# Moving every third state product of a selective scan from VectorE to GpSimd, and folding the layer norms, in a decoder layer on one core

## The chip, the cores and the metric

The kernel runs on one core of a Trainium2 chip. The metric is the device time of one execution in microseconds; the times of several runs are given by their median. The core has TensorE (PE, matrix products into PSUM), VectorE (DVE), ScalarE (ACT), GpSimd (POOL) and SyncE (SP, which here only issues DMAs). Each engine works through its own list of instructions in order and waits on semaphores.

## What is computed

One decoder layer in fp32, batch 4, length 512, width 512, with three residual branches:

```python
x = x + attn(_layernorm(x))                  # chunked linear attention, 16 heads of 32
x = x + mixer(ctx_1024, _layernorm(x))       # selective scan, gated by silu of the normed x
x = x + ffn(_layernorm(x))                   # bit-linear feed-forward, hidden 2048
# the mixer's recurrence, 16 states n for each of 512 channels:
dA    = exp(dt * A);  state = state * dA + (dt * u) * B[n];  y = sum_n(state * C[n])
y     = (y + D * u) * silu(z)
# bit_linear: rows of x are scaled by 127 / max|x| and rounded before the product
```

## The kernel before

Each batch row b (0 to 3 in the code; the text says rows 2 to 4 for b = 1 to 3) goes through a front (input projection, convolution, step sizes dt), the scans with the attention beside them, and the mixer gate and feed-forward. `step(b, f)` on every engine interleaves the scans and the attention of row b with the mixer end and feed-forward of row f = b - 1; `first_row` and `last_row` are the ends. The order on each engine is written out: the tables `STEP_PIECES` (VectorE's halves of a unit), `STEP_DECAYS` (ScalarE) and `STEP_SPREADS` (TensorE) say how many pieces of the recurrence are taken at each named point of the list.

A *unit* is one state n for one half h of the channels, 128 partitions x 2 x 512 columns; there are 32 per row, `unit(u)` gives (b, h, n) of unit u = 32 b + j. In rows b = 1 to 3 the order is states 0 to 5 of half 0, then states 6 to 15 with both halves one after the other (`joined`: the second uses the same B and C rows), then states 0 to 5 of half 1: 22 distinct rows of B and C for 32 units. For each unit:

- ScalarE forms the decay exp(dt A) into one of four DEC buffers (L1353).
- TensorE broadcasts B's row n to 128 partitions into a PSUM bank of PB by a product (L1060), once for each distinct row, when the scan that used the bank before is done.
- VectorE multiplies DU (dt u) by it into PSUM (`inputs_b`, L1893) and then scans: W = scan(decay, PB) (`scan`, L1904). W is a ring of four SBUF buffers; scan u waits until the transfer of unit u - 4 has landed.
- SyncE loads C's row n as a broadcast into one of two CROW buffers (`c_row`), two units ahead.
- GpSimd multiplies W by it in place (`outputs_c`, L1730), waits until the transfer before has landed (`y_summed`) and issues the DMA that adds W to ACC in SBUF (L1743). In row b = 0 two units are added first. GpSimd also forms DU (`step_inputs`, L1751), splits B for the broadcast product (`split`), and adds the output bias after unit 7 of a row (`bias`, L1718).

Norms. The next row's input is normed by VectorE in attention group 3: bn_stats (L1835), aggregation (L1841), ScalarE's reciprocal root (`rstd`), then four in-place tensor_scalar (`normed`, L1848), transposed by TensorE. The mixer's gate needs the mean and variance of X1 right after the residual additions (`residual`, L2104; `mixer_sums`; `aggregate(f, 1)`; `gate_shift`; ScalarE's `gate_z`, L1405), and then VectorE multiplies ACC by it (`gate_mixer`, L2115; in the last row `gate_tile`, L1966). For the feed-forward `add_mixer` (L2120) forms X2, bn_stats follow, `normed` writes OT, and `row_scales` (in the last row `tile_scales`) takes the largest magnitude (L2009, L1977) for the rounding.

## Time and profile before

| | us |
|---|---|
| median of 3 runs | 931.2 (930.08 to 934.58) |
| profiled execution, its own time | 933.21 |
| its span | 931.4 |

| engine | busy us | share |
|---|---|---|
| TensorE, matrix products | 791.9 | 85% |
| VectorE | 780.5 | 84% |
| ScalarE | 584.6 | 63% |
| GpSimd | 489.2 | 53% |

The span is the time from the first to the last instruction of the profiled execution. A share of busy time is an average over stages; an engine below 100% may still be the one that everything waits for in a stage. In rows of the trace "out<-in" names the tiles with buffer numbers left out, and an arrow in brackets names what ended the idle time before an instruction.

### The profile page before, as it was taken

How to read it: one execution, taken by the hardware profiler on the slowest of the kernel's cores; microseconds unless marked ns; L12 is line 12 of the kernel's file. 1: busy time of each engine (PE TensorE's matmuls, PEld its weight loads, DVE VectorE, ACT ScalarE, POOL GpSimd, SP SyncE). 2: the span in 40 equal slices, each digit the busy share in tenths (PEclk: the TensorE clock that was granted, in tenths of full speed). 3: DMA queues.
4: the chain of work that ended last, by engine and by line, in shares of the span. 5: the costliest groups of instructions: out<-in, count | busy, mean ns of one | idle time of the engine just before them, and what ended most of it. 6: DMA issues, size and time to landing. Idle time of an engine off the chain costs nothing. (4 is left out here: it accounts for less than half of the span.)

```text
span 931.4 us, 11695 instructions
## 1 busy us (share of the span) xinstructions
PE 791.9 (85%) x4070; PEld 429.4 (46%) x4070; DVE 780.5 (84%) x913; ACT 584.6 (63%) x868; POOL 489.2 (53%) x292
## 2 busy tenths in 40 slices
PE   5859898369887888998978987998889899999798
PEld 1334555143452334665443333656445335664343
DVE  5887788996998986989699988589788998988875
ACT  3788899965647866445365866453455796453552
POOL 0456678786646523575447643276444755565020
PEclk8889997679789999989999999989998999999999
DMA  8687788866546535666534563456643565666000
GB/s 291 252 247 224 229 251 225 238 187 165 122 96 133 114 69 113 143 144 169 125 68 113 121 140 68 111 130 149 158 98 79 123 126 130 151 144 135 1 12 34
DMA packets 50781, 131.12 MB, mean 141 GB/s; under 512 B 7298, under 2 KB 7874, under 8 KB 50724
## 3 DMA queue, kind: packets, MB, share of 16 engines
q0 software_dynamic: 16128, 58.73, 33.4%
q1 hardware_dynamic: 34596, 71.65, 23.8%
q8 instruction: 33, 0.54, 0.2%
q14 instruction: 24, 0.20, 0.1%
HBM read 67.09 MB, written 4.35 MB: 77 GB/s over the span
## 5 line engine op out<-in xcount | busy, mean ns | idle before, releaser
L1730 POOL TENSOR_TENSOR W<-W,CROW 128x1024 f32<-128x1024 f32 x128 | 321.9, 2531 | 160.1 <-DVE W L1904 132.6
L1904 DVE TENSOR_TENSOR_SCAN W<-DEC,PB 128x1024 f32<-128x1024 f32 x125 | 285.1, 2281 | 10.2 <-ACT DEC L1353 4.0
L1743 POOL DMA_DIRECT2D ACC<-W x112 | 98.3, 878 | 155.1 <-DMA ACC<-W 132.0
L1893 DVE TENSOR_TENSOR PB<-DU,PB 128x1024 f32<-128x1024 f32 x128 | 156.5, 1223 | 13.7 <-PE PB L1060 10.1
L1353 ACT ACTIVATE DEC<-DT,ACOL 128x511 f32<-128x511 f32 x250 | 160.1, 710 | 11.5 <-DVE W L1904 11.4
L1116 PE MATMUL bank<-W,ARENA 128*128 128x512 fp8e4 x512 | 124.0, 386 | 0.0
L1308 ACT ACTIVATE ARENA<-bank 128x512 f32<-128x512 f32 x56 | 32.5, 592 | 73.4 <-PE bank L876 36.4
L1116 PEld LDWEIGHTS bank<-W,ARENA 128*128 128x128 bf16 x512 | 45.3, 98 | 61.2 <-issue 16.9
L1451 ACT ACTIVATE ARENA<-bank,SDQ 128x512 f32<-128x512 f32 x64 | 43.4, 685 | 46.0 <-PE bank L1116 45.8
L1060 PE MATMUL PB<-BC,ID 96*128 96x512 bf16 x98 | 39.3, 415 | 33.7 <-DVE W L1904 32.4
L876 PE MATMUL bank<-XNT,WK 128*128 128x512 f32 x128 | 63.7, 644 | 2.2 <-DVE ARENA L1936 2.2
L1936 DVE TENSOR_TENSOR ARENA<-bank,CAUSAL 128x512 f32<-128x512 f32 x64 | 42.5, 680 | 24.4 <-PE bank L977 24.3
L938 PEld LDWEIGHTS bank<-WV,XNT 128*128 128x128 f32 x512 | 60.5, 195 | 3.2 <-issue 2.2
L2044 DVE SCALAR_TENSOR_TENSOR ARENA<-bank,SDQ,ARENA 128x512 f32<-128x512 f32 x64 | 47.3, 743 | 17.3 <-PE bank L1116 6.6
L876 PE MATMUL bank<-XNT,WQ 128*128 128x512 f32 x128 | 61.4, 624 | 0.0
L938 PE MATMUL bank<-WV,XNT 128*128 128x128 f32 x512 | 61.2, 278 | 0.3 <-ACT ARENA L1440 0.3
L1132 PE MATMUL bank<-W,ARENA 128*128 128x512 fp8e4 x256 | 57.9, 379 | 0.0
L1109 PE MATMUL bank<-BROW,RT 32*128 32x512 bf16 x128 | 30.2, 388 | 23.7 <-DVE ARENA L2044 14.0
L1860 DVE SCALAR_TENSOR_TENSOR U<-bank,CW,U 128x511 f32<-128x511 f32 (+2 forms) x48 | 35.5, 747 | 15.1 <-ACT U L1315 13.8
L1751 POOL TENSOR_TENSOR DU<-DT,U 128x512 f32<-128x512 f32 x16 | 22.9, 1506 | 47.2 <-ACT DT L1333 47.2
L1440 ACT ACTIVATE ARENA<-bank 128x512 bf16<-128x512 int16 x76 | 40.5, 594 | 11.0 <-PE bank L918 10.9
L876 PE MATMUL bank<-ARENA,FM 128*128 128x512 f32 x96 | 45.5, 609 | 0.0
(175 smaller groups left out, 1333.2 us busy)
## 6 DMA issues: line engine op xcount, KB each, us to landing
ACC<-W POOLq DMA_DIRECT2D x112, 512.0 KB, 4.6
CROW<-c_rows SPq DMA_DIRECT2D x98, 256.0 KB, 3.6
W<-in_wffn SPq DMA_DIRECT2D x27, 512.0 KB, 6.2
X<-in_wffn SPq DMA_DIRECT2D x21, 512.0 KB, 5.8
X<-in_x SPq DMA_DIRECT2D x7, 1024.0 KB, 8.6
out_dram<-X SPq DMA_DIRECT2D x16, 256.0 KB, 2.2
X<-in_ctxT SPq DMA_DIRECT2D x4, 512.0 KB, 5.6
ARENA<-in_x SPq DMA_DIRECT2D x1, 1024.0 KB, 5.6
```

What stands on the lines that cost most here:

```text
L876: last = pe.matmul(o, lhs, rhs, start=start, stop=n == len(terms) - 1)
L938: last = pe.matmul(o[:, t * P:(t + 1) * P], XNT[:, k, t * P:(t + 1) * P], WV[:, k, g * P:(g + 1) * P], start=k == 0, stop=k == KT - 1)
L1116: last = pe.matmul(o, XQT[:, k, t * P:(t + 1) * P], w, start=False, stop=k == KT - 1)
L1132: last = pe.matmul(o, HT[:, k, :], W8[:, 2 * WPC + k // 2, (k % 2) * 512:(k % 2) * 512 + 512], start=k == 0, stop=k == HK - 1)
L1353: last = act.activation(to[:, i, 1:], DT[:, e, 1:], ACT.Exp, scale=ACOL[:, e, n:n + 1])
L1451: act.activation(G[n % 2], R.bank(f, "G", t, c)[:, :], ACT.Silu, scale=SDQ[:, 0, t:t + 1])\
L1730: pool.tensor_tensor(w, w, CROW[k % 2][:, :].unsqueeze(1).broadcast_to([P, 2, L]), ALU.mult)\
L1743: pool.dma_start(ACC[accumulator(u)][:, :, :], w, accum_op=ALU.add).then_inc(y_summed, 16)
L1893: dve.tensor_tensor(into, du, rows, ALU.mult).then_inc(dbu_done.sem, 1)
L1904: dve.tensor_tensor_scan(flat(W[u % 4]), flat(decay_of(u)), flat(PB[:, scan_bank(u):scan_bank(u) + 2, :]), 0.0, ALU.mult, ALU.add).then_in ...
L1936: dve.tensor_tensor(homes(b, g)["st"][c % 2].rearrange("p (h q) -> p h q", h=HPG), R.bank(b, "S", g, c)[:, :].rearrange("p (h q) -> p h q" ...
L2044: dve.scalar_tensor_tensor(h, R.bank(f, "V", t, c)[:, :], SDQ[:, 1, t:t + 1], G[(t * HC + c) % 2], ALU.mult, ALU.mult)\
```

## The change

In rows b = 1 to 3 every third distinct row of B is handled by GpSimd: SyncE loads it as a broadcast row from DRAM into one buffer BRW (`b_row`, four units ahead; B rows are now stored to DRAM beside C's), GpSimd multiplies DU by it straight into W (`inputs_b` on GpSimd, two units ahead of its multiplication by C), and VectorE scans W in place. TensorE's broadcast and VectorE's product fall away for those 10 of 32 units of a row. The other units keep their way; the tables that order the pieces are as before.

The norms: the next input is normed on ScalarE by a scaled Identity. The mixer's mean comes from the residual addition itself (tensor_tensor_reduce, with the sum), the variance from a ScalarE Square with accumulation. Before the feed-forward, `add_mixer` also keeps the row minimum, and the normalisation also keeps its maximum, so that the largest magnitude needs no reduction of its own. Small tiles are packed together, and the bias columns lie in ARENA, which changes no instruction.

```diff
+POOL_EVERY = 3
+POOL_AHEAD = 2
+ROW_AHEAD = 4
+def on_pool(u):
+    return u >= UNITS and (ROW_OF[u] - ROW_OF[u // UNITS * UNITS]) % POOL_EVERY == POOL_EVERY - 1
...
+        BRW = sb("BRW", [P, L])
...
+            def b_row(u):
+                if u >= TOTAL or not on_pool(u) or joined(u):
+                    return
+                b, _, n = unit(u)
+                k = POOL_ROW[u]
+                sp.wait_ge(*bc_stored.at(b))
+                if k > 1:
+                    sp.wait_ge(pool_dbu_done, BY_POOL[LAST_IN_POOL_ROW[k - 1]])
+                sp.dma_start(BRW[:, :], bc_rows[b, n].partition_broadcast(P)).then_inc(b_loaded, 16)
...
-                sp.dma_start(c_rows[b], XBC[N:2 * N, :]).then_inc(c_stored.sem, 16)
+                sp.dma_start(bc_rows[b], XBC[0:2 * N, :]).then_inc(bc_stored.sem, 16)
...
+                    b_row(b * UNITS + j + ROW_AHEAD)
                     if b * UNITS + j + 2 < TOTAL:
                         c_row(b * UNITS + j + 2)
...
-                    if not joined(u):
+                    if not joined(u) and not on_pool(u):
                         spread_b(u)
...
+            def deviations(f, t):
+                act.wait_ge(*mean_ready.at(f, t + 1))
+                act.activation(Z[:, t, :], X1[:, t, :], ACT.Square, bias=NMEAN[:, t:t + 1],
+                               accum_out=VAR[:, t:t + 1]).then_inc(var_ready.sem, 1)
...
+            def normed(b):
+                act.wait_ge(*xshift_ready.at(b))
+                for t in range(TT):
+                    act.activation(XROWS[b][:, t, :], XROWS[b][:, t, :], ACT.Identity, bias=XSHIFT[:, t:t + 1],
+                                   scale=RSTD[0][:, t:t + 1]).then_inc(xn_ready.sem, 1)
...
+            def inputs_b(u):
+                b, h, n = unit(u)
+                if opens(u):
+                    pool.wait_ge(*du_ready.at(b, 2 * h + 2))
+                if u - 4 < PAIRED and u % 2 == 0:
+                    pool.wait_ge(pair_added, (u - 4) // 2 + 1)
+                else:
+                    pool.wait_ge(y_summed, 16 * transfers(u - 4))
+                pool.wait_ge(b_loaded, 16 * POOL_ROW[u])
+                pool.tensor_tensor(W[u % 4][:, :, :], DU[:, 2 * h:2 * h + 2, :],
+                                   BRW[:, :].unsqueeze(1).broadcast_to([P, 2, L]), ALU.mult).then_inc(pool_dbu_done, 1)
...
             for u in range(TOTAL):
+                if u + POOL_AHEAD < TOTAL and on_pool(u + POOL_AHEAD):
+                    inputs_b(u + POOL_AHEAD)
                 outputs_c(u)
...
+            def normed_peak(f, t):
+                dve.tensor_tensor_reduce(OT[:, t, :], X2[:, t, :], MV[1][:, t, 0:1].broadcast_to([P, D]),
+                                         RSTD[1][:, t:t + 1], -LARGEST, ALU.subtract, ALU.max, HIGH[:, t:t + 1])\
+                   .then_inc(xn2_ready.sem, 1)
...
+            def scan_in_place(u):
+                dve.wait_ge(pool_dbu_done, BY_POOL[u])
+                dve.wait_ge(*da_ready.at(0, u + 1))
+                dve.tensor_tensor_scan(flat(W[u % 4]), flat(decay_of(u)), flat(W[u % 4]), 0.0,
+                                       ALU.mult, ALU.add).then_inc(scan_done.sem, 1)
...
-                    if n % 2:
+                    if n % 2 and on_pool(n // 2):
+                        scan_in_place(n // 2)
+                    elif n % 2:
                         scan(n // 2)
-                    else:
+                    elif not on_pool(n // 2):
                         inputs_b(n // 2)
...
-                dve.tensor_reduce(AMX[:, :], OT[:, :, :], AX.X, ALU.max, apply_absolute_value=True)\
-                   .then_inc(q_step.sem, 1)
+                dve.wait_ge(*deep_step.at(f))
+                dve.tensor_tensor(AMX[:, :], DEEP[:, :], HIGH[:, :], ALU.max).then_inc(q_step.sem, 1)
...
-                dve.tensor_tensor(X1[:, t, :], R.bank(f, "wo", t)[:, :], X1[:, t, :], ALU.add)\
+                dve.tensor_tensor_reduce(X1[:, t, :], R.bank(f, "wo", t)[:, :], X1[:, t, :], 1.0, 0.0,
+                                         ALU.add, ALU.add, TOTALS[:, t:t + 1])\
...
-                dve.tensor_tensor(X2[:, t, :], R.bank(f, "yT", t)[:, :], X1[:, t, :], ALU.add)\
+                dve.tensor_tensor_reduce(X2[:, t, :], R.bank(f, "yT", t)[:, :], X1[:, t, :], 1.0, LARGEST,
+                                         ALU.add, ALU.min, LOW[:, t:t + 1])\
...
-            def mixer_sums(f, t):
+            def mixer_mean(f, t):
                 dve.wait_ge(*R.drained_at(f, "wo", t))
-                sums(f, 1, X1, t)
+                dve.tensor_scalar(NMEAN[:, t:t + 1], TOTALS[:, t:t + 1], -1.0 / D, None, ALU.mult)\
+                   .then_inc(mean_ready.sem, 1)
```

## Rows read from the trace of the kernel before

**Rows 1.** Busy time by stage: from, to, length, then each engine, clock, DMA share.
```profile
229.80:458.00 228.20, 198.83 (x1020) 107.94 (x1019) 196.60 (x218) 130.55 (x196) 125.34 (x78) 0.95 0.57 125
458.00:678.00 220.00, 194.27 (x1003) 106.31 (x1002) 185.81 (x203) 129.39 (x194) 113.20 (x72) 0.93 0.53 117
678.00:851.40 173.40, 160.59 (x938) 91.61 (x937) 158.37 (x176) 106.28 (x157) 97.26 (x59) 0.98 0.57 124
851.40:931.40 80.00, 69.78 (x361) 31.09 (x359) 57.09 (x137) 36.79 (x61) 9.08 (x7) 0.98 0.11 27
```

**Rows 2.** The chain of waits from 527 to 931 us, by line, as shares.
```profile
by line: PE bank L876 17.2%; PE bank L1116 10.5%; issue 6.5%; PE bank L1017 5.2%; PE bank L1132 5.2%; DVE W L1904 5.0%; PE bank L938 4.5%; PE bank L977 3.4%; PE bank L1000 2.9%; DVE PB L1893 2.9%; DVE HAM L2052 2.6%; DVE BST L1835 2.5%; PE 
```

**Rows 3.** Pieces of the same chain in order of time: start, length, what.
```profile
643.58 1.84 DVE X L1848 x3
645.55 2.96 issue
682.11 1.19 DVE BST L1835 x2
```

**Rows 4.** Who waited for whom, GpSimd, 229 to 852 us: total, times, longest.
```profile
POOL ACC L1743 <- DMA ACC<-W: 125.1, 64, 6.1
POOL W L1730 <- DVE W L1904: 119.5, 31, 14.0
POOL ACC L1743 <- POOL W L1730: 14.3, 26, 0.6
```

**Rows 5.** Groups of instructions: shapes, count, busy us, mean ns, idle before.
```profile
L1730 POOL TENSOR_TENSOR W<-W,CROW 128x1024 f32<-128x1024 f32 x128 | 321.9, 2531 | 160.1 <-DVE W L1904 132.6 <-DMA CROW<-c_rows 27.5
L1904 DVE TENSOR_TENSOR_SCAN W<-DEC,PB 128x1024 f32<-128x1024 f32 x125 | 285.1, 2281 | 10.2 <-ACT DEC L1353 4.0 <-issue 3.0 <-DMA ACC<-W 1.0
L1893 DVE TENSOR_TENSOR PB<-DU,PB 128x1024 f32<-128x1024 f32 x128 | 156.5, 1223 | 13.7 <-PE PB L1060 10.1 <-issue 2.1
L1060 PE MATMUL PB<-BC,ID 96*128 96x512 bf16 x98 | 39.3, 415 | 33.7 <-DVE W L1904 32.4 <-DVE BC L1877 1.3
```

**Rows 6.** Timeline of VectorE and GpSimd near 245 us: start, length, what.
```profile
244.67 3.42 DVE L2115 TENSOR_TENSOR ARENA<-ACC,ARENA 128x1024 f32<-128x1024 f32 x2
245.09 4.13 POOL L1751 TENSOR_TENSOR DU<-DT,U 128x512 f32<-128x512 f32 x2 [2.62 <-ACT DT L1333]
```

**Rows 7.** Groups of the norms; the last is a line's durations, minimum/median/maximum.
```profile
L1835 DVE BATCH_NORM_STATS2 BST<-X 128x6 f32<-128x512 f32 x44 | 28.8, 681 | 0.3
L1848 DVE TENSOR_SCALAR X<-X,MV,RSTD 128x512 f32<-128x512 f32 x12 | 13.4, 1172 | 0.0
L2104 DVE TENSOR_TENSOR X<-bank,X 128x512 f32<-128x512 f32 x16 | 10.8, 678 | 13.2 <-PE bank L1023 13.2
L1848 DVE TENSOR_SCALAR OT<-X,MV,RSTD 128x512 f32<-128x512 f32 x12 | 7.2, 661 | 0.0
L2009 DVE TENSOR_REDUCE AMX<-OT 128x4 f32<-128x2048 f32 x3 | 6.8, 2283 | 0.1
L1491 ACT ACTIVATION_READ_ACCUMULATOR W<-W 128x1 f32 x18 | 3.4, 189 | 0.0
L1393 ACT ACTIVATE OT<-bank x16: 576/588/597, 104.2 to 843.6; 128x512 f32<-128x512 f32 x16
```

**Rows 8.** Timeline around the bias addition of step b = 2.
```profile
497.11 0.88 POOL L1743 DMA_DIRECT2D ACC<-W  x1 [0.54 <-issue]
497.71 4.81 POOL L1718 TENSOR_TENSOR X<-X,OUTB 128x2048 f32<-128x2048 f32 x1
507.23 2.29 DVE L1904 TENSOR_TENSOR_SCAN W<-DEC,PB 128x1024 f32<-128x1024 f32 x1
```

**Rows 9.** Timeline of GpSimd, its last two DMA issues.
```profile
851.51 0.88 POOL L1743 DMA_DIRECT2D ACC<-W  x1 [1.53 <-DMA ACC<-W]
856.29 0.88 POOL L1743 DMA_DIRECT2D ACC<-W  x1 [1.52 <-DMA ACC<-W]
```

**Rows 10.** Timeline of VectorE in the last row, the gate's second pair.
```profile
862.79 1.40 DVE L1966 TENSOR_TENSOR ARENA<-ACC,ARENA 128x512 f32<-128x512 f32 x2 [1.39 <-ACT ARENA L1405]
```

More of the change, by code:

```diff
@@ L615, in homes @@
             return at
+        BIAS, BREST = (part((HID // 64) * i, HID // 64) for i in range(2))
+        BPART = part(HID // 32, 3 * HID // 128, bf16).rearrange("p (j n) -> p j n", j=3)
         BCR = X1[0:32, 0, :]
@@ L1526, in attention @@
                         square(b, g - 1)
+                    if b + 1 < BATCH and g == GROUPS - 1:
+                        normed(b + 1)
                     decays(b, "a", g, 1)
@@ L1568, in first_row @@
                 rstd(0, 0)
+                normed(0)
                 act.wait_ge(setup_v, SETUP_V - 2)
@@ L1601, in step @@
                     decays(b, "r", 2)
+                for t in range(TT):
+                    deviations(f, t)
                 rstd(f, 1)
@@ L1680, in last_row @@
                 for pair in range(2):
+                    for t in (2 * pair, 2 * pair + 1):
+                        deviations(f, t)
                     rstd_tiles(f, 1, 2 * pair, 2 * pair + 2)
@@ L2145, in attention @@
                     units(b, "a", g, 0)
+                    if b + 1 < BATCH and g == GROUPS - 1:
+                        norm_shift(b + 1)
                     feature(b, g, 1)
                     units(b, "a", g, 1)
[L2148 to L2149 removed]
                     units(b, "a", g, 2)
@@ L2232, in step @@
                 feature(b, 0, 1)
-                normed(f, 2, X2, xn2_ready)
+                normed_peaks(f)
                 units(b, "v", 9)
```

167 lines of the change are left out of this document (94 added, 73 removed).

## The prediction, made before any run of the changed kernel

> **What bounds the kernel now.** I read the busy time by stage first, then the chain of waits, then who waits for whom, then single durations. The stages [rows 1] are the steps that interleave the scans of row b with the feed-forward part of row b-1: 228.2, 220.0 and 173.4 us for b = 1, 2, 3, then 80 us of the last row alone. Over the three steps (621.6 us) TensorE is busy 553.7 us, VectorE 540.8, ScalarE 366.2, GpSimd 335.8. Neither of the first two is full; each waits for the other in turn. The chain that ended last says which of them matters where: from 527 us on, its lines [rows 2] are mostly TensorE's; added up over its listed pieces, TensorE holds 219 of those 404 us and VectorE 81. So a microsecond taken off TensorE there is worth roughly 0.6, one off VectorE 0.2 to 0.3, unless it lies where VectorE is the chain. Such places exist: around the norms [rows 3] the chain runs through VectorE. By contrast in the last attention stretch (790 to 851 us) VectorE holds 3 us of the chain and TensorE 54.
>
> GpSimd looks idle, but its chain is stiffer than its busy share. It waits 125.1 us for its own accumulating transfers and 119.5 us for scans between 229 and 852 us [rows 4]. Each transfer into ACC waits for the one before; in a backlog the issues are 4.78 us apart [rows 9] whatever GpSimd does. 32 units at that pace are 153 us of a step.
>
> **Part 1, a third of the products moved to GpSimd.** Of the 22 distinct states per row, numbers 2, 5, 8, 11, 14, 17, 20 move: 2 + 6 + 2 = 10 of 32 units, 30 in all, with 21 of TensorE's B broadcasts.
> - VectorE loses 30 products of 1223 ns [rows 5], 36.7 us.
> - TensorE loses 21 x 0.415 us [rows 5] = 8.7 us.
> - GpSimd gains 30 products shaped like its multiplication by C, 2.53 us [rows 5]: 76 us. In a backlog its cycle is 4.78 us, of which 1.52 is waiting before the issue [rows 9]; 0.55 of that (14.3 us in 26 waits [rows 4]) would remain as the wait for its own multiplication. So about 1.0 us of a new product hides and 1.4 lengthens the chain: 14 us a row if it were always in backlog.
> - The scan in place now reads both inputs from SBUF. The only VectorE instructions of the trace with that trait are the two Z products (L2115). At 244.67 us such a pair took 3.42 us [rows 6], where two products of that size are 2.4 [rows 5], while GpSimd's pair of 512-column products beside it took 4.13 us, where half the size of two multiplications is 2.5: one engine waits until the other's instruction ends, in both directions. The Trainium skill (SBUF — State Buffer, Who interferes with whom) says this as a rule: a VectorE instruction with two SBUF inputs contends with a GpSimd instruction that reads SBUF, and the second to issue blocks fully. By that rule, the trace agrees. This speaks against the change. GpSimd will be in a reading instruction about (336 - 84 + 76)/610 = 54% of the time (84 us being its 96 DMA issues of 0.88 us [rows 9]); the mean remainder of 2.5 us is 1.25 us, so 0.67 us per scan; since GpSimd often starts just behind a scan, I take 0.8 us: 24 us for 30 scans. Bounds: 0, and a whole multiplication each, 30 x 2.53 = 76 us. A scan that only reads other memory keeps its 2.28 us.
> - New waits. VectorE's scan in place waits for GpSimd's product, with all of VectorE's list (masks, features, gated products, and behind them TensorE) behind it. GpSimd forms it two units ahead, before multiplication u. Mostly it is done 2 to 4 us before the scan. The exception is after GpSimd's 4.81 us bias addition in step b = 2 [rows 8]: it ends at 502.5, then product 74 (2.4), multiplication 72 (2.4), an issue (0.6) and product 75 (2.4) end near 510, where the scan of unit 75 starts at 507.2 now [rows 8]: 3 us, and some 1 us at 74. In b = 1 and 3 scans are later relative to the bias. The wait for the ring (scan u waits for transfer u-4; that of unit 75 for the issue of 497.11, landed some 4.6 us later, 5.5 us before the scan [rows 8]) has 5 to 10 us to spare in most attention stretches, paired in this way, and is eaten by chain delays of 5 to 9 us there.
> - SyncE: 21 broadcast loads of a B row (256 KB each) go ahead of the C row loads. Their own wait, for the previous GpSimd row's product, is older than the wait of the C row queued behind it, so it holds up nothing; the store of 32 rows instead of 16 costs nothing visible. If a load is late, GpSimd's whole queue waits for it; in b = 1 and 2 it sits, like the C row of unit 20, behind a result store.
>
> On the path: products, L1893 holds 2.9% of the 404 us of chain [rows 2], 11.7 us, of some 52 products (65 us) run in it, 18%; so -36.7 x 0.18 = -6.6. Blocking: L1904 holds 5.0%, 20 us of some 121, 17%: +24 x 0.17 = +4.1. Broadcasts: -8.7 x 0.62 = -5.4. Sum -7.9.
>
> **Part 2, the norms.**
> - The next input's normalisation (L1848, X<-X) leaves VectorE: 12 instructions, 13.4 us [rows 7], a mean of 1172 ns because some sat blocked beside GpSimd; at 643.5 us they and the gap of 2.96 us hold the chain for 5.3 us [rows 3]. The same four cost ScalarE about 0.6 to 0.8 us each (its Square: 588 ns median [rows 7]), beside VectorE's work; ScalarE is busy only 59% in the steps [rows 1]. On the path I take half: -6.7 for three rows.
> - Statistics of the mixer's input: 16 of the 44 bn_stats (681 ns [rows 7], 0.60 apart [rows 3]) and 16 aggregations go, 16 means of some 0.15 us come, ScalarE adds 16 squares of 0.59 us with an accumulator read of 0.19 [rows 7]. At the start of a step the chain has two bn_stats and the aggregation behind the last residual [rows 3], 1.19 + 0.4 us; in their place come one mean, one square and its read, 0.9: -0.7 each, and about -0.3 each for the shorter run of residuals. -3 for three steps, nothing in the last row, where one bn_stats is traded for one square.
> - Rounding scale: the normed X2 (12 in 7.2 us) and the maximum over 2048 (3 of 2283 ns [rows 7]) become four instructions with a row maximum. No tensor_tensor_reduce is in the trace. Nearest rows: a tensor_tensor of 512 columns is 0.68 us [rows 7]; the scan needs 2.28 us where a product of its size needs 1.22 [rows 5], so 1.2 us is the other end. An accumulator read may add up to 0.19 us (ScalarE's). I take 0.78. Per step 4.7 us become 3.1 + 0.4 of small ones + 0.7 blocked (its mean operand is in SBUF too): -0.5, three times -1.5. Last row: 0.60 (7.2/12) and a quarter of 2.28 become 0.78 + 0.15, four times: -1.
> - The residual and mixer additions gain the reduction as well: 32 x 0.1 = 3.2 us of VectorE, on the path +1.2.
> Sum -11.
>
> **Part 3, what GpSimd gives back.** Step b = 2: +2 of the 4 us of waiting. At the end of b = 3 GpSimd's last issue is at 856.29 [rows 9], lands near 861 (the previous one left at 851.51 and the wait for it ended just before 856.29), and VectorE needs ACC at 862.79 [rows 10]: 1.9 us of slack. Four of the last twelve units (units 22, 23, 27, 30 of the row) are GpSimd's, 4 x 1.4 = 5.6 us, less the slack and an earlier start: +3. Late scans at the ends of b = 1 and 2: +2. Sum +7.
>
> Total -7.9 - 11 + 7 = -12. The profiled execution took 933.2 (span 931.4), 2 us above the median of 931.2, so its forecast is 921 and the median's 919.
>
> **The rivals.**
> - *Slower: GpSimd's chain becomes the bound.* Each moved unit costs the 1.4 us above and 1.8 of the 2.3 us during which a scan in place can hold GpSimd off, 3.2 us. In each row's attention stretch some four such units stand where GpSimd never waits for a scan: 13 us less 6 of slack in the ring, +7 for b = 1 and 2, and at the very end without slack, 7 + 7 + 13 = +27 in place of my +7: 939. It decides from about 2.8 us (12 units x 2.8 less 14 of slack is the 19 us gained elsewhere) of chain per moved unit. For: the cadence of 4.78 us is already met at the end of b = 3 [rows 9]. Against: 119.5 us of waiting for scans [rows 4]. Chance 0.15.
> - *Hidden anyway.* VectorE's savings fall where TensorE ends last, as in 790 to 851 us. Then only the broadcasts (-5.4) and some 4 us of norms count, against +7: 929. Chance 0.14.
> - *The reducing form takes two cycles per column.* 48 instructions x 0.55 = 26 us of VectorE, 40% on the path, +10: 929. The Trainium skill (Vector Engine (DVE) Microarchitecture Reference, Points that are easy to get wrong) says that the accumulating form with two SBUF sources that aren't bf16 runs at half rate; no row shows that form. That would strike only the 16 of the normed X2, in place of all 48. Chance 0.07.
> - *No blocking.* If scans in place meet a free GpSimd, the 4.1 and most of the 7 vanish, and freed VectorE time starts later work sooner: 907. Chance 0.06.
> - *It does not do what it says*, the products arriving after the scan wants them, ends in the slower rival, whose 0.15 holds it.
>
> **How the numbers follow.** The forecast, 906 to 926, has 0.58. The bounds: blocking from 0 to 76 us is -4 to +9 on the path, the reducing form up to +10, GpSimd's part 0 to +20, the norms -20 to -5. Range 902 to 938. A change under 0.5% (926.5 to 935.9) can't be told from none. Faster: 0.58 + 0.06 less the forecast's own edge 0.02, 0.62. Same: 0.14 + 0.07, 0.21. Slower: 0.15 + 0.02, 0.17.
>
> **What would show it.** Scans in place: 2.28 us where GpSimd is quiet, 3 to 4.9 where it isn't, mean about 3.1; any that stay at 2.28 throughout refute the blocking. GpSimd busy near 560 us, its wait for scans well under 119.5. VectorE busy near 745, TensorE near 783. tensor_tensor_reduce at 0.7 to 0.8 us. VectorE waiting for a GpSimd product near unit 75 and hardly elsewhere. The last ACC transfer later relative to the last scan. The prediction is wrong if the reducing form is slow, if waits for the product are frequent, or if the steps b = 1 and 2 shrink by over 10 us each.

## The result and the profile after

The changed kernel takes 972.8 us (median of 4 runs, 969.45 to 975.81) where the kernel before took 932.6 on the same chip: ratio 1.043, interval 1.040 to 1.046. It was forecast at 919, with a range up to 938. It is 40 us slower, and the forecast missed in sign. Two kernels below had one slow execution (3379 us beside 941 to 948 for the norms alone, 952 beside 938 to 944 without GpSimd's products), which their medians leave out here and which the 944.9 and 941.2 in later expectations hold.

First the busy time of the engines, from the page of the changed kernel (span 969.5 us):

```profile
PE 804.8 (83%) x4049; PEld 434.0 (45%) x4049; DVE 769.3 (79%) x906; ACT 607.6 (63%) x916; POOL 569.6 (59%) x322
```

VectorE lost 11 us of work, not the 35 forecast; TensorE, with 21 broadcasts fewer, is busy 13 us longer. Then the stages, cut at the first residual addition of a row (columns as in [rows 1]: TensorE's products, its weight loads, VectorE, ScalarE, GpSimd, granted clock, DMA share, GB/s; the first line is row 1):

```profile
0.00:239.10 239.10, 173.44 (x755) 93.96 (x756) 180.27 (x176) 186.94 (x268) 147.35 (x81) 0.83 0.77 226
239.10:474.40 235.30, 198.14 (x1004) 108.36 (x1003) 194.31 (x209) 136.66 (x208) 151.80 (x87) 0.91 0.57 127
474.40:702.70 228.30, 198.84 (x1003) 107.11 (x1002) 181.03 (x205) 134.87 (x206) 136.06 (x79) 0.92 0.52 118
702.70:885.80 183.10, 164.74 (x931) 93.10 (x930) 159.92 (x177) 109.25 (x165) 122.77 (x70) 0.94 0.57 126
885.80:969.50 83.70, 69.62 (x360) 31.43 (x358) 53.74 (x144) 39.92 (x69) 11.67 (x9) 0.96 0.14 32
```

[Rows 1] end their first three stages at 458, 678 and 851.4; here they end at 474.4, 702.7 and 885.8. Row 1 ended at 229.8 and now ends at 239.1. So every stage lost: 9 us in row 1, 34.4 - 9.3 = 25 in the three steps, 4 in the tail. (In the kernel before, the first residual addition of row 2 is at 454.5, not at the 458 where [rows 1] cut; with that cut the steps grew by 10.5, 4.7 and 9.8 us.) The loss of row 1 comes with the norms: its end is at 237.2 with the norms alone and at 230.5 with the products alone, the two kernels of the next section. TensorE's granted clock was 0.93 to 0.98 in the steps [rows 1] and is 0.91 to 0.94, and its busy time there rose from 554 to 562 us. I take that for an effect of the waiting; no run separates the two. The instructions that answer to [rows 5], and the new ones (L2004 is the scan in place, L1817 GpSimd's product):

```profile
L1792 POOL TENSOR_TENSOR W<-W,CROW 128x1024 f32<-128x1024 f32 x128 | 325.4, 2558 | 126.1 <-DVE W L1997 94.0 <-DMA CROW<-bc_rows 18.4 <-DVE W L2004 13.7
L1997 DVE TENSOR_TENSOR_SCAN W<-DEC,PB 128x1024 f32<-128x1024 f32 x95 | 216.7, 2281 | 15.2 <-DMA ACC<-W 5.4 <-ACT DEC L1395 4.5 <-POOL W L1803 2.7
L2004 DVE TENSOR_TENSOR_SCAN W<-DEC,W 128x1024 f32<-128x1024 f32 x30 | 106.9, 3562 | 15.3 <-POOL W L1817 14.7 <-ACT DEC L1395 0.6
L1817 POOL TENSOR_TENSOR W<-DU,BRW 128x1024 f32<-128x1024 f32 x30 | 81.5, 2717 | 4.7 <-DMA BRW<-bc_rows 4.7
```

A scan in place takes 3562 ns on average, one from PSUM 2281. Of GpSimd's 132.6 us of waiting for scans [rows 5] 108 are left. The chain of waits between 812 and 905 us. In the kernel before, TensorE's lines held 56 of those 93 us and GpSimd's none:

```profile
by line: POOL W L1792 32.1%; issue 24.7%; POOL W L1817 12.5%; DMA ACC<-W 11.2%; POOL ACC L1805 7.3%; DVE W L1997 2.5%; PE bank L1162 1.9%; PE bank L1064 1.4%; ACT DEC L1395 1.3%; PE bank L906 0.9%; DVE ARENA L2068 0.8%; DVE BST L1914 0.7%; 
```

From 819 to 890 us the chain never leaves GpSimd. Its "issue" pieces are mostly its waits for the transfer before.

### The profile page after: what moved, and what is told of

The parts are those of the page before. It is cut to its first block and busy times, and to the rows that moved or that the text cites. A ratio compares the mean times of both kernels' runs of the same rounds, so it can differ in the third digit from the quotient of the medians.

```text
span 969.5 us, 11793 instructions
## 1 busy us (share of the span) xinstructions
PE 804.8 (83%) x4049; PEld 434.0 (45%) x4049; DVE 769.3 (79%) x906; ACT 607.6 (63%) x916; POOL 569.6 (59%) x322
## 5 line engine op out<-in xcount | busy, mean ns | idle before, releaser
L1792 POOL TENSOR_TENSOR W<-W,CROW 128x1024 f32<-128x1024 f32 x128 | 325.4, 2558 | 126.1 <-DVE W L1997 94.0
L1997 DVE TENSOR_TENSOR_SCAN W<-DEC,PB 128x1024 f32<-128x1024 f32 x95 | 216.7, 2281 | 15.2 <-DMA ACC<-W 5.4
L1395 ACT ACTIVATE DEC<-DT,ACOL 128x511 f32<-128x511 f32 x250 | 160.1, 711 | 9.3 <-DVE W L2004 8.8
L1986 DVE TENSOR_TENSOR PB<-DU,PB 128x1024 f32<-128x1024 f32 x98 | 119.6, 1221 | 17.4 <-PE PB L1090 14.3
L1146 PE MATMUL bank<-W,ARENA 128*128 128x512 fp8e4 x512 | 131.8, 404 | 0.0
L2004 DVE TENSOR_TENSOR_SCAN W<-DEC,W 128x1024 f32<-128x1024 f32 x30 | 106.9, 3562 | 15.3 <-POOL W L1817 14.7
L1817 POOL TENSOR_TENSOR W<-DU,BRW 128x1024 f32<-128x1024 f32 x30 | 81.5, 2717 | 4.7 <-DMA BRW<-bc_rows 4.7
L906 PE MATMUL bank<-XNT,WQ 128*128 128x512 f32 x128 | 63.2, 640 | 1.6 <-ACT XNT L1338 1.6
L906 PE MATMUL bank<-XNT,WK 128*128 128x512 f32 x128 | 62.6, 635 | 1.9 <-DVE ARENA L2038 1.8
L1162 PE MATMUL bank<-W,ARENA 128*128 128x512 fp8e4 x256 | 57.9, 379 | 0.0
L1828 POOL TENSOR_TENSOR DU<-DT,U 128x512 f32<-128x512 f32 x16 | 26.0, 1663 | 44.9 <-ACT DT L1375 44.9
L1090 PE MATMUL PB<-BC,ID 96*128 96x512 bf16 x77 | 31.6, 423 | 25.0 <-DVE W L1997 23.7
L1047 PE MATMUL bank<-WO,OT 128*128 128x512 f32 x96 | 44.4, 615 | 5.9 <-DVE OT L2045 5.9
```

Of the source, the lines that this page charges most:

```text
L906: last = pe.matmul(o, lhs, rhs, start=start, stop=n == len(terms) - 1)
L1146: last = pe.matmul(o, XQT[:, k, t * P:(t + 1) * P], w, start=False, stop=k == KT - 1)
L1162: last = pe.matmul(o, HT[:, k, :], W8[:, 2 * WPC + k // 2, (k % 2) * 512:(k % 2) * 512 + 512], start=k == 0, stop=k == HK - 1)
L1395: last = act.activation(to[:, i, 1:], DT[:, e, 1:], ACT.Exp, scale=ACOL[:, e, n:n + 1])
L1792: pool.tensor_tensor(w, w, CROW[k % 2][:, :].unsqueeze(1).broadcast_to([P, 2, L]), ALU.mult)\
L1817: pool.tensor_tensor(W[u % 4][:, :, :], DU[:, 2 * h:2 * h + 2, :], BRW[:, :].unsqueeze(1).broadcast_to([P, 2, L]), ALU.mult).then_inc(pool ...
```

## The experiments

All ratios are to the kernel before, with 95% intervals; 1% is 9.3 us. L numbers differ a little from kernel to kernel; the names tell what is meant.

### The two parts alone

Norms without products:

```diff
-    return u >= UNITS and (ROW_OF[u] - ROW_OF[u // UNITS * UNITS]) % POOL_EVERY == POOL_EVERY - 1
+    return False
```

> All of the change except the products: no unit goes to GpSimd, so the B rows are broadcast by TensorE and multiplied by VectorE as before. Prediction as recorded: norms are worth -11 us, so 922. Theory 'products' (all of the loss beyond the start comes with the moved products): the norms gain their 11 us in rows 2 to 4 but lose some 6 us in row 1, where the normed input now stands on ScalarE ahead of the first decay, so 927 (ratio 0.995). Rival 'norms' (the small two-input instructions gate_shift and norm_shift, blocked up to 4.7 us beside GpSimd, and the longer ScalarE list cost more than the norms gain): over 938 (ratio over 1.005).

Measured: 942.1 us, 1.0127 (1.0081 to 1.0174). The rival holds in its number: the norms, forecast at -11, alone cost 12 us. Which of its two causes it is comes next.

Products without norms (every norm edit of the diff undone):

> All of the change except the norms: the norms are as before, 10 of 32 units in rows 2 to 4 are GpSimd's products with the scan in place. Prediction as recorded: -7.9 + 7, so 932. Theory 'products': 973 less the 6 us of the start and plus the norms' gain of 11, so about 975 (ratio 1.045). Rival 'norms': under 950 (ratio under 1.02).

Measured: 965.2 us, 1.0358 (1.0324 to 1.0391). It lies between the two expectations: the products alone cost 33 us, and both parts lose.

### What the norms lose on

The first row's input normed on VectorE again, no products:

```diff
                 rstd(0, 0)
-                normed(0)
...
-                norm_shift(0)
+                for t in range(TT):
+                    dve.tensor_scalar(XROWS[0][:, t, :], XROWS[0][:, t, :], MV[0][:, t, 0:1], RSTD[0][:, t:t + 1],
+                                      ALU.subtract, ALU.mult).then_inc(xn_ready.sem, 1)
```

> The norms alone (no GpSimd products), with the first row's input normed on VectorE as in the kernel before; the later rows' still on ScalarE. Theory 'start' (the 14 us between 931 and 945 begin at the ScalarE norm ahead of the first decays, which pushes row 1 by 2 to 7 us): 936 to 938, row 1 back at 230 us, and the rest of the kernel no faster than before. Rival (row 1 regains the time at its DMA-bound places): 943 to 946, as without this edit.

Then every row's:

> The norms alone, with every input norm on VectorE as before: what is left is the mixer's mean from the residual addition with ScalarE's square, and the rounding scale without its own reduction. Prediction: -3 - 2.5 + 1.2 = -4, so 927. Theory 'ScalarE' (the input norm on ScalarE is the losing part, since it stands in ScalarE's list ahead of decays and TensorE's transposes): 926 to 931, below the kernel with the first norm alone on VectorE. Rival 'mixer part' (the square behind the mean delays the gate): 935 or more.

And, with the first row's on VectorE, the other rows' still on ScalarE but later in its list:

```diff
-                    if b + 1 < BATCH and g == GROUPS - 1:
-                        normed(b + 1)
                     decays(b, "a", g, 1)
...
                     decays(b, "a", g, 2)
+                    if b + 1 < BATCH and g == GROUPS - 1:
+                        normed(b + 1)
```

> The norms alone, first row's input norm on VectorE (939.9 us so far), and for the other rows ScalarE's four Identities three groups of decays later in attention group 3, behind instead of ahead of the decays that the next scans want. Theory 'place' (ScalarE waits at the Identity for VectorE's norm_shift, 3 us at 172 in that kernel, and VectorE's next scan then waits 4.2 us for its decay): 929 to 933, as with every norm on VectorE (930.3). Rival 'engine' (the Identities cost the same wherever they stand, or the small norm_shift blocked 1.8 to 4.6 us beside GpSimd is the cost): 937 to 942.

| norms alone, input norm | us | ratio |
|---|---|---|
| all rows on ScalarE | 942.1 | 1.0127 (1.0081 to 1.0174) |
| first row on VectorE | 939.9 | 1.0089 (1.0058 to 1.0120) |
| and the others' later on ScalarE | 934.2 | 1.0030 (0.9998 to 1.0063) |
| all rows on VectorE | 930.3 | 0.9987 (0.9965 to 1.0009) |

By the ratios the steps are 3.5, 5.5 and 4 us. The first is smaller than its interval, the other two just clear of theirs, and the ends are well apart: the whole loss of the norms, 13 us, is the input norm on ScalarE, with what waits behind it. Of the 9.5 us of the later rows, 5.5 are its place in ScalarE's list. Of the three expectations above, only that of 930.3 was met (926 to 931): 939.9 lies between the start theory's 938 and its rival's 943, and 934.2 lies 1 us above the place theory's 933. The start theory also wanted row 1 back at 230 us. It ends at 235.9 with the first row's norm on VectorE, and at 228.8 only when the norm of row 2, near 172 us, is later too. So the larger part of row 1's loss is that second norm (one profile of each). What happens there shows in the trace of the kernel with the first row on VectorE (timeline of VectorE and ScalarE; L1924 is `norm_shift`, L1550 the Identity, L1395 the decays), and below it the same decays in the kernel before:

```profile
172.07 1.78 DVE L1924 SCALAR_TENSOR_TENSOR TILES<-MV,ROOTS 128x4 f32<-128x4 f32 x1
...
173.89 2.93 ACT L1550 ACTIVATE X<-X,TILES,ROOTS 128x512 f32<-128x512 f32 x4 [2.99 <-DVE TILES L1924]
...
176.72 3.76 ACT L1395 ACTIVATE DEC<-DT,ACOL 128x511 f32<-128x511 f32 x6
```

```profile
170.47 3.77 ACT L1353 ACTIVATE DEC<-DT,ACOL 128x511 f32<-128x511 f32 x6
```

ScalarE stands 2.99 us before a VectorE instruction of 128x4 elements, works 2.93 us on the norm, and the six decays that stand behind both start 6.25 us later. Who waited for whom over that whole kernel (total, times, longest):

```profile
ACT X L1550 <- DVE TILES L1924: 12.0, 3, 4.6
DVE W L1996 <- ACT DEC L1395: 6.6, 4, 4.2
```

and with the norm later in ScalarE's list:

```profile
DVE W L1996 <- ACT DEC L1395: 3.6, 2, 3.0
ACT X L1550 <- DVE TILES L1924: 1.6, 1, 1.6
```

In the first row the norm stands ahead of the decays at the very start. The changed kernel, then the kernel before:

```profile
34.36 2.92 ACT L1550 ACTIVATE ARENA<-ARENA,TILES,ROOTS 128x512 f32<-128x512 f32 x4 [0.98 <-DVE TILES L1925]
37.19 2.54 ACT L1395 ACTIVATE DEC<-DT,ACOL 128x511 f32<-128x511 f32 x4
37.34 2.75 PE L936 MATMUL bank<-IDF,ARENA 128*128 128x128 f32 x16 [2.23 <-ACT ARENA L1550]
...
43.13 6.38 PE L906 MATMUL bank<-XNT,WQ 128*128 128x512 f32 x8 [1.57 <-ACT XNT L1338]
```

```profile
33.39 2.54 ACT L1353 ACTIVATE DEC<-DT,ACOL 128x511 f32<-128x511 f32 x4
...
36.13 1.97 PE L906 MATMUL bank<-IDF,ARENA 128*128 128x128 f32 x16 [0.91 <-DVE ARENA L1848]
...
39.90 3.67 PE L876 MATMUL bank<-XNT,WQ 128*128 128x512 f32 x8
```

The decays start 3.8 us later. The eight products for q (L906 and L876, `XNT,WQ`) start 3.2 us later and take 6.38 us in place of 3.67, after TensorE had stood idle for 2.23 us ahead of the transposes and 1.57 us ahead of them, and they end 5.9 us later. The granted clock was lower there (windows, columns as in [rows 1]); 37 to 50 us of the changed kernel, then 36 to 44 of the kernel before:

```profile
37.00:50.00 13.00, 10.65 (x28) 5.65 (x29) 10.47 (x7) 12.91 (x24) 7.72 (x3) 0.61 0.40 125
```

```profile
36.00:44.00 8.00, 6.60 (x28) 3.87 (x29) 7.90 (x7) 7.97 (x15) 3.09 (x2) 1.00 0.50 140
```

These 28 matmuls ran at 0.61 of the full 2.4 GHz (part of the time at 1.2) in place of 1.00: 4.05 us more of TensorE's time. The gaps alone do not decide it. With the norms alone the same two gaps, 2.20 and 1.55 us, stand there, the q products come at 42.36 and take 3.67 us as before, and 37 to 50 us has a clock of 0.87:

```profile
42.36 3.67 PE L906 MATMUL bank<-XNT,WQ 128*128 128x512 f32 x8 [1.55 <-ACT XNT L1338]
```

### What the products lose on: a table of two by two

The scans of the moved units take their second operand from one PSUM column, so that they have one SBUF input; everything else of the change stays:

```diff
-                dve.tensor_tensor_scan(flat(W[u % 4]), flat(decay_of(u)), flat(W[u % 4]), 0.0,
+                dve.tensor_tensor_scan(flat(W[u % 4]), flat(decay_of(u)),
+                                       PB[:, 1, 0:1].broadcast_to([P, 2 * L]), 0.0,
```

> As the changed kernel, but the 30 scans that were in place take their second operand from one PSUM column instead of W, so they have one SBUF input only; GpSimd still forms every product and the scans still wait for it (the scanned values are wrong, the work of every engine is the same). Theory 'blocking' (the 38 us that the 30 scans run over 2.28 us each, and what GpSimd is held off by them, is the cause): scans at 2.3 us throughout and 940 or less (ratio to before at most 1.01). Rival 'GpSimd's list' (the 76 us of added products lengthen GpSimd's chain of multiplications and transfers, whoever reads what): 955 to 970 (ratio 1.025 to 1.04) though the scans are at 2.3.

GpSimd's products left out, the scans still in place (the loads of B rows go on, and wait for a scan in place of a product):

```diff
-                if u + POOL_AHEAD < TOTAL and on_pool(u + POOL_AHEAD):
-                    inputs_b(u + POOL_AHEAD)
...
-                dve.wait_ge(pool_dbu_done, BY_POOL[u])
+                dve.wait_ge(y_summed, 16 * transfers(u - 4))
```

> As the changed kernel, but GpSimd's 30 products are left out: the scan in place waits for the ring (transfer of unit u - 4) and scans what W holds. B rows are loaded all the same. The scan still has two SBUF inputs. Theory 'blocking': scans in place are still 3.5 us or so beside GpSimd's multiplications by C and the time stays above 945 (ratio over 1.015). Rival 'GpSimd's list': with its list as short as before, 915 to 930 (ratio under 1).

Both edits together:

> As the changed kernel, but GpSimd's 30 products are left out and the 30 scans take their second operand from one PSUM column: VectorE's 30 products and TensorE's 21 broadcasts are gone at no price. With the norms alone at 944.9, the changed kernel at 972.8, GpSimd's products without blocked scans at 951.2 and blocked scans without GpSimd's products at 941.2, this is the fourth corner. The prediction's saving of the products (-6.6 - 5.4 on the path): 933. Theory 'sum' (the two costs, 21 to 28 us of blocking and 24 to 31 us of GpSimd's list, add up): 972.8 - 21.6 - 31.6 = 919.6. Rival 'each feeds the other' (blocking costs more when GpSimd's list is long, since GpSimd then reads at any moment): 930 to 936, so that the two costs alone are 8 and 18 and together 40.

And two kernels in which GpSimd works as much, but VectorE doesn't wait for it: the product goes to a tile of its own, once with scans in place and once with the PSUM column:

```diff
-                pool.wait_ge(b_loaded, 16 * POOL_ROW[u])
-                pool.tensor_tensor(W[u % 4][:, :, :], DU[:, 2 * h:2 * h + 2, :], BRW[:, :]...
+                pool.tensor_tensor(SPARE[:, :, :], DU[:, 2 * h:2 * h + 2, :], OUTB[:, :]...
...
-                dve.wait_ge(pool_dbu_done, BY_POOL[u])
+                dve.wait_ge(y_summed, 16 * transfers(u - 4))
```

> The changed kernel, but GpSimd's 30 products are written to a tile of their own (from OUTB in place of the loaded B row, whose loads fall away; bf16), so that VectorE's scan in place waits for the ring, not for a product: the scan still has two SBUF inputs and GpSimd still works 76 us more. The kernel with both and with the wait took 972.8; without blocking but with the wait 951.2; with blocking but without products 941.2. Theory 'wait for the product' (14.7 us of VectorE's waits and what stands behind them; the scan queued behind a late product is what makes blocking dear): 945 to 955. Rival 'two readers' (the same instructions hold each other off, whoever waits for whom): 965 to 973.

> As the run before, and the 30 scans take their second operand from one PSUM column: GpSimd's load alone, with neither the wait for its product nor a blocked scan. Free products gave 938.8, the load with the wait 951.2. Theory 'wait for the product': 939 to 943, so that nearly all of the 12.4 us is the wait. Rival 'GpSimd's chain' (later multiplications, later transfers, later ring): 948 to 952.

| GpSimd forms the products | scan with one SBUF input | scan with two |
|---|---|---|
| no | 938.8, 1.0079 (1.0047 to 1.0111) | 938.3, 1.0140 (1.0066 to 1.0215) |
| yes, nobody waits for them | 945.0, 1.0152 (1.0121 to 1.0183) | 970.8, 1.0422 (1.0393 to 1.0452) |
| yes, the scan waits | 951.2, 1.0207 (1.0163 to 1.0251) | 972.8, 1.0431 (1.0398 to 1.0464) |

(The top and the bottom row load the B rows, the middle row does not; the norms are the change's in all.) The ratio at the top right, 1.0140, has a wide interval and lies above what its three ordinary executions give: by medians, without the one of 952 us, that kernel is at 1.008 and its neighbour at 1.007. With one SBUF input all scans took 2.28 us, as all theories had it. Most expectations missed. The first kernel (951.2) is between its two, 940 and 955; the second (top right) is under the 945 of the one and over the 930 of the other; the third, for which the sum of the two prices would have given 920, came out at 939, even above the 930 to 936 of the theory that each feeds the other; the last (945.0) is between its two. Only the fourth, 970.8, lies inside one, the two readers' (965 to 973), and far from the other, 945 to 955.

Over the top left corner, 1.0079, two SBUF inputs alone cost 0.6% at most and by medians 0.1%, GpSimd's load alone 0.7%, both together 3.4%, 32 us. The remaining 2.1%, 20 us (by the four intervals together some 0.9% either way), belong to neither but to both at once. The wait for the product, the suspect for which the last two were made, costs 0.1% to 0.6%, the loads of the B rows included: that theory fell. The rival, two readers that hold each other off, stands.

The groups of the two kernels of the middle row tell how. Two SBUF inputs, then one (L1785 is the multiplication by C, L1811 the product, L1822 GpSimd's DU):

```profile
L1785 POOL TENSOR_TENSOR W<-W,CROW 128x1024 f32<-128x1024 f32 x128 | 332.0, 2604 | 125.0 <-DVE W L1991 88.7 <-DMA CROW<-bc_rows 25.3 <-DVE W L2001 10.8
L2001 DVE TENSOR_TENSOR_SCAN W<-DEC,W 128x1024 f32<-128x1024 f32 x30 | 103.8, 3459 | 0.9 <-ACT DEC L1388 0.9
L1811 POOL TENSOR_TENSOR SPARE<-DU,OUTB 128x1024 bf16<-128x1024 f32 x30 | 84.8, 2826 | 0.0
L1822 POOL TENSOR_TENSOR DU<-DT,U 128x512 f32<-128x512 f32 x16 | 26.0, 1663 | 46.6 <-ACT DT L1368 46.6
```

```profile
L1785 POOL TENSOR_TENSOR W<-W,CROW 128x1024 f32<-128x1024 f32 x128 | 326.5, 2567 | 116.8 <-DVE W L1991 86.6 <-DMA CROW<-bc_rows 24.6 <-DVE W L2001 5.6
L2001 DVE TENSOR_TENSOR_SCAN W<-DEC,PB 128x1024 f32<-128x1024 f32 x30 | 68.3, 2275 | 2.7 <-DMA ACC<-W 1.8 <-ACT DEC L1388 0.9
L1811 POOL TENSOR_TENSOR SPARE<-DU,OUTB 128x1024 bf16<-128x1024 f32 x30 | 79.6, 2655 | 0.0
```

VectorE is held off 103.8 - 68.3 = 35.5 us, GpSimd 5.5 + 5.2 = 10.7 us in its multiplications and products, and 4.3 in forming DU (21.7 us with one SBUF input). Without GpSimd's products the scans in place lose less, 92.0 us against 68.2, and GpSimd's multiplications nothing (322.3 us against 323.2), first with two inputs:

```profile
L1793 POOL TENSOR_TENSOR W<-W,CROW 128x1024 f32<-128x1024 f32 x128 | 322.3, 2529 | 158.0 <-DVE W L1995 100.7 <-DMA CROW<-bc_rows 40.3 <-DVE W L2005 16.9
L2005 DVE TENSOR_TENSOR_SCAN W<-DEC,W 128x1024 f32<-128x1024 f32 x30 | 92.0, 3067 | 0.5 <-ACT DEC L1396 0.5
```

So 24 us of blocking cost at most 6 us where GpSimd's multiplications have slack (158 us of waiting), and 35 + 11 us cost 25 where they have less (125). That the second is dear because both engines are then late for each other in turn is my reading of the next view, not a run of its own. Timeline of the changed kernel near 858 us:

```profile
855.33 0.88 POOL L1805 DMA_DIRECT2D ACC<-W  x1 [2.19 <-DMA ACC<-W]
855.94 2.66 POOL L1817 TENSOR_TENSOR W<-DU,BRW 128x1024 f32<-128x1024 f32 x1
858.25 2.64 POOL L1792 TENSOR_TENSOR W<-W,CROW 128x1024 f32<-128x1024 f32 x1
858.63 4.42 DVE L2004 TENSOR_TENSOR_SCAN W<-DEC,W 128x1024 f32<-128x1024 f32 x1 [3.51 <-POOL W L1817]
861.43 0.88 POOL L1805 DMA_DIRECT2D ACC<-W  x1 [0.55 <-POOL W L1792]
862.04 3.15 POOL L1792 TENSOR_TENSOR W<-W,CROW 128x1024 f32<-128x1024 f32 x1
```

VectorE waits 3.51 us for the product. GpSimd's next instruction stands right behind the product and is already running when the scan is let go at 858.63: the scan sits through all of it, 4.42 us for a scan of 2.28. Then the scan holds off GpSimd's next multiplication, 3.15 for 2.64 us. The issue behind the product (861.43, of the unit two ahead of the moved one) comes 6.1 us after the one before, where the cadence in a backlog was 4.78 [rows 9].

### Fewer units, another place, another norm

Every sixth B row in place of every third, 4 units a row in place of 10, and the full number of units for comparison, both with the input norms on VectorE:

> As the run with every input norm on VectorE, but every sixth distinct B row in place of every third is GpSimd's: 4 units a row in place of 10. Against the kernel without GpSimd products (930.3). Theory 'each feeds the other' (the cost grows faster than the number of moved units, since blocking alone and GpSimd's load alone cost 2.5 and 12.4 while together they cost 34): under 6 us, 930 to 936. Rival 'a price per unit' (28 us for 30 units, 0.93 us each): 12 units cost 11, so 941.

> The whole change with every input norm on VectorE as before. Theory 'norm place and products add up': 972.8 - 14.6 = 958. Rival 'they share their waits' (the products fill ScalarE's lateness, so that the norms cost less beside them, as the kernel with the products alone at 965.2 suggests: 972.8 - 965.2 = 7.6): 963 to 967.

Measured: 943.0 us, 1.0137 (1.0109 to 1.0165), for 12 units, and 967.4, 1.0392 (1.0362 to 1.0422), for 30. Over the kernel with no moved unit (0.9987) that is 1.5% or 14 us, 1.17 us a unit, and 4.05% or 38 us, 1.26 a unit. Within its interval (0.9 to 1.4 us for the 12 units) the price is per unit; that 12 units would cost under 6 us fell. Two more follow. The norm's 1.4% and the products' 4.05% do not add up to the 4.3% of the whole: with the products there, the norm on ScalarE costs 0.4%, within its interval of nothing. That the two share waits, the rival's reason, fits this, and no run tests it apart. And moving units loses at both numbers tried.

The product between the multiplication by C and the issue:

```diff
                     .then_inc(hc_done.sem, 1)
+                if u + POOL_AHEAD < TOTAL and on_pool(u + POOL_AHEAD):
+                    inputs_b(u + POOL_AHEAD)
                 b, h, n = unit(u)
```

> The whole change, but GpSimd forms each product between its multiplication by C and the issue of that unit's transfer, in place of ahead of the multiplication. The same work; the product then lies where GpSimd waits for the transfer before. Theory 'GpSimd's list' (1.4 us of chain per moved unit): 955 to 965. Rival 'blocking' (what counts is how long GpSimd reads beside the scans, which this does not change) and 'the product is on the path of the issue' : 970 to 980.

Measured: 990.5 us, 1.0631 (1.0582 to 1.0679), 18 us worse than the change and outside both expectations. The gap before an issue in a backlog holds 1.5 us [rows 9] and a product takes 2.7, so the issue behind one is late: GpSimd waits 85 us for transfers before its issues where the changed kernel waits 111. But the product is later for its scan too: VectorE waits 27.0 us for products in place of 14.7, and GpSimd 156 us for scans in place of 108. Which of the two costs more is not shown.

### The small instructions

`gate_shift` and `norm_shift` with one SBUF tensor and a per-partition scalar, in the changed kernel:

```diff
-                dve.tensor_tensor(NMR[:, :], NMEAN[:, :], RSTD[1][:, :], ALU.mult)\
-                   .then_inc(nmr_step.sem, 1)
+                for t in range(TT):
+                    ins = dve.tensor_scalar(NMR[:, t:t + 1], NMEAN[:, t:t + 1], RSTD[1][:, t:t + 1], None, ALU.mult)
+                ins.then_inc(nmr_step.sem, 1)
```

> The changed kernel, but gate_shift and norm_shift, each one VectorE instruction on 128x4 with two SBUF inputs, are four of 128x1 that read one SBUF tensor and take the other factor as a per-partition scalar. Theory 'small ones block' (they took 9.1 us in 3 and 6.7 us in 4 instructions, 4.2 and 4.7 of it at the start of the steps where the chain goes through them): every one at about 0.15 us, and 963 to 968. Rival (the wait is only moved to the next instruction, or a scalar read from SBUF blocks as well): 970 to 975.

What had been seen in the changed kernel (groups, then the timeline near 708 us):

```profile
L2214 DVE TENSOR_TENSOR TILES<-TILES,ROOTS 128x4 f32<-128x4 f32 x3 | 9.1, 3040 | 6.1 <-ACT ROOTS L1369 6.1
L1925 DVE SCALAR_TENSOR_TENSOR TILES<-MV,ROOTS 128x4 f32<-128x4 f32 x4 | 6.7, 1664 | 0.2 <-ACT ROOTS L1369 0.2
```

```profile
707.88 2.65 POOL L1817 TENSOR_TENSOR W<-DU,BRW 128x1024 f32<-128x1024 f32 x1
708.12 4.74 DVE L2214 TENSOR_TENSOR TILES<-TILES,ROOTS 128x4 f32<-128x4 f32 x1 [2.03 <-ACT ROOTS L1369]
710.19 2.64 POOL L1792 TENSOR_TENSOR W<-W,CROW 128x1024 f32<-128x1024 f32 x1
```

With one SBUF tensor each:

```profile
L1926 DVE TENSOR_SCALAR TILES<-MV,ROOTS 128x1 f32<-128x1 f32 x16 | 2.3, 203 | 0.2 <-ACT ROOTS L1369 0.2
L2217 DVE TENSOR_SCALAR TILES<-TILES,ROOTS 128x1 f32<-128x1 f32 x12 | 1.7, 207 | 6.1 <-ACT ROOTS L1369 6.1
```

15.8 us of VectorE's time became 4.0; the time 966.8, 1.0388 (1.0347 to 1.0429), inside the expected 963 to 968 and some 4 us less, which the intervals just don't separate from none. At 708.12 an instruction of 512 elements waits for the product's end and then for the whole multiplication behind it. A product directly ahead of a multiplication makes such pairs, which is one way in which GpSimd's load can feed the blocking. The pairs exist without products too: with the norms alone and the first row on VectorE, `norm_shift` waited through GpSimd's two DU products and a multiplication.

```profile
647.97 2.78 POOL L1827 TENSOR_TENSOR DU<-DT,U 128x512 f32<-128x512 f32 x2
648.48 4.59 DVE L1924 SCALAR_TENSOR_TENSOR TILES<-MV,ROOTS 128x4 f32<-128x4 f32 x1
650.41 2.63 POOL L1791 TENSOR_TENSOR W<-W,CROW 128x1024 f32<-128x1024 f32 x1
```

Nor is one SBUF tensor always enough. In the kernel before, the input norm reads one SBUF tensor and two per-partition scalars over 512 columns and took from 0.53 to 3.42 us, the longest beside a multiplication:

```profile
L1848 DVE TENSOR_SCALAR X<-X,MV,RSTD x12: 533/536/3421, 175.7 to 648.5; 128x512 f32<-128x512 f32 x12
```

Last, the version that the runs point to: no products, every input norm on VectorE, and these small instructions by column.

> No GpSimd products, every input norm on VectorE (930.3 in the runs so far, 0.9987 of before), and gate_shift and the two small subtractions ahead of the rounding scale as 128x1 instructions with one SBUF tensor each (they took 2.6, 2.6 and 0.94 us blocked in that kernel). Theory: 2 to 4 us less, ratio 0.995 to 0.998. Rival (VectorE is not what these places wait for): 0.998 to 1.001.

Measured: 930.2 us, 0.9986 (0.9965 to 1.0007). Not to be told from the kernel before, nor from 0.9987 without the columns: the rival's range, and the small instructions gain nothing where GpSimd has no products.

## Why the prediction was wrong, point by point

- **The sum.** Forecast: -12 for the savings, +4 for blocking, +7 for GpSimd, -11 for the norms. Measured, by ratios: -4.5 for the savings, +32 for blocking and GpSimd's load together, +1 for the wait and the B rows' loads, +12 for the norms, which is the 40 us. Two steps failed: the 17% by which blocking was brought to the path, apart from GpSimd's load, and the input norm on ScalarE, taken as a gain.
- **What bounds the kernel.** That TensorE and VectorE wait for each other in turn was right, and "GpSimd's chain is stiffer than its busy share" too. The argument then let only the end of row 4 feel it.
- **Savings of the products, -12.** Free of every price they are worth 1.0127 - 1.0079 = 0.5%, 4.5 us, with intervals that overlap. Weighting each removed microsecond by its engine's share of the chain overstated them. VectorE worked 29 us less (755.4 to 726.4), and its waits grew in many places, for ScalarE's and TensorE's results in the feed-forward and the attention; its wait for the broadcasts, 17.0 us and then 15.1, did not.
- **Blocking, 24 us of VectorE, +4 on the path.** The mechanism was right. The size was 30 x (3.562 - 2.281) = 38 us, inside the bounds 0 and 76. The conversion was the failed step: 17% of it on the path. With GpSimd loaded, two SBUF inputs cost 2.2% (1.0431 - 1.0207) or 2.7% (1.0422 - 1.0152), 21 to 25 us. The weight was taken from scans that nobody held off; a held-off scan stands where GpSimd is reading, and, as I read it, what is queued on GpSimd is then late in turn. The line that L2115 is the only VectorE instruction with two SBUF inputs was also wrong: `gate_tile` (L1966) and `gate_shift` (L2109, 128x4, 0.16 to 2.16 us in the kernel before) are others, and the last shows that a small one is held off too. The rule of the Trainium skill (SBUF — State Buffer, Who interferes with whom) that the second to issue blocks fully is what the row at 858.63 shows. The row at 708.12 adds that a waiting VectorE instruction can be passed over when the first GpSimd instruction ends and another one is ready.
- **GpSimd gives back, +7.** GpSimd's load without blocked scans costs 0.7% to 1.3% (1.0152 and 1.0207 less 1.0079), 7 to 12 us. That term was near. That the two terms were costed apart and added was the gap: about 20 us.
- **Waits for the product.** Forecast 4 us near unit 75 and hardly elsewhere; 14.7 us in 9 waits came. Dropping them gains 0.1% beside blocked scans.
- **Norms, -11.** The -6.7 for the input norm on ScalarE was +13 (1.0127 - 0.9987 is 1.4%): 9.5 for the three later rows, and some 3.5 for the first row's, which stood in no term. The step counted busy time ("the same four cost ScalarE about 0.6 to 0.8 us each": 0.80 was right) and that ScalarE has room, 59%. It did not ask what is queued behind them, which the text itself asks of every added wait: decays for the next scans. The other two norm terms, -3 - 2.5 + 1.2 = -4, measured -0.1% (-0.35% to +0.09%), so -1 us: nothing that can be told from zero.
- **The reducing form.** Taken at 0.78 us; 742, 687 and 677 ns, and some 80 for each read of the accumulator. The row of the 16 normed X2, whose operands X2 and the mean both lie in SBUF in fp32:

```profile
L1930 DVE CUSTOM_DVE_ANT_0 OT<-X,MV,ROOTS 128x512 f32<-128x512 f32 x16 | 11.5, 742 | 0.0
L2208 DVE CUSTOM_DVE_ANT_0 X<-bank,X 128x512 f32<-128x512 f32 x16 | 10.9, 687 | 13.2 <-PE bank L1053 12.8
```

  The Trainium skill (Vector Engine (DVE) Microarchitecture Reference, Points that are easy to get wrong) says that the instruction shape `S2S2D2_STT` with two SBUF sources that aren't bf16 halves its throughput. The prediction took tensor_tensor_reduce for that shape. The trace lists it as a custom instruction, and whether it has the shape no row tells. Measured, the first row, with both sources in SBUF, takes 742 ns and the second, which reads PSUM, 687: it isn't at half the rate.
- **The rivals.** "GpSimd's chain becomes the bound" came nearest, at 0.15, and 939 was too low. It charged 3.2 us for four units a row, those in the attention stretches, and saw slack for the others; the price is 1.2 us for each of 30 units, and the three steps lose alike (with every input norm on VectorE, they are 9.7, 12.0 and 9.9 us longer with moved units than without, from one first residual addition to the next). The chances stood 0.62 for faster because the blocking's bounds were carried to the path with one weight, at both ends (-4 to +9). With the weight at 1 the upper end would have been +76.
- **What would show it.** Scans in place at 2.28 us where GpSimd is quiet and up to 5.2 elsewhere, mean 3.56 (3.1 forecast); GpSimd busy 570 us (560 forecast), its wait for scans down. That much was right. VectorE 769 in place of 745: 14 us more of blocked scans and 9 + 7 us in small blocked instructions that the text didn't list are more than the difference. Of the signs of being wrong only the waits for products came; that the steps might grow was none of them. TensorE 805 in place of 783, with the mean granted clock at 0.903 where it had been 0.930; a longer TensorE was in no term.

## What to carry to other kernels

Before moving work to an engine with idle time, ask of each moved instruction what stands behind it in that engine's list and who waits for that; busy shares of 53% (GpSimd) and 63% (ScalarE) hid a serial chain in one and decays on the path in the other. An instruction of VectorE with two SBUF inputs must be costed together with GpSimd's load, not beside it: here two SBUF inputs alone cost at most 6 us, GpSimd's load alone 7, both together 32. Where a small one has a form of one column with one SBUF tensor and a per-partition scalar, that form wasn't held off here (28 of them at 0.18 to 0.22 us), though what it gains in time is not clear of nothing.

## What the runs showed of the hardware

- A VectorE instruction with two SBUF inputs is not spared by being small: 128x4 took 0.16 us alone and 4.74 beside a product and a multiplication of GpSimd.
- At the end of a GpSimd instruction, GpSimd's next one, if it is ready, can go ahead of the VectorE instruction that already waits (708.12 through 707.88 and 710.19; 648.48 through 647.97 and 650.41). It doesn't always: in the pairs of [rows 6] the second VectorE product got its turn between the two of GpSimd, which itself had just been held off (245.80 to 248.09, where GpSimd's second ran from 246.97 to 249.22). What decides it no run shows. A scan in place took up to 5.2 us in the changed kernel.
- One SBUF tensor with per-partition scalars was held off at 128x512 (0.53 us alone, up to 3.42 beside GpSimd) and not at 128x1 (0.18 to 0.22 us).
- A scan whose second operand is one PSUM column takes 2275 ns, as one that reads 1024 columns of PSUM (2283 in the same kernel).
- 28 matmuls at the start took 10.65 us of TensorE's time at a granted clock of 0.61 and 6.60 at 1.00. Before the first of these stretches TensorE had gaps of 2.23 and 1.57 us, before the second one of 0.91; but behind gaps of 2.20 and 1.55 us, with the norms alone, the eight q products took 3.67 us, as in the kernel before. What set the clock is open.
